# A four-layer graph kernel: two fp32 products become three rounded passes each, two tiles share a buffer, and the written-out order is redrawn

## The reference, cut to what matters

```
w  = adj * exp((x Wq0 + bq)(x Wk0 + bk)^T);  x = LN(x + (w / rowsum(w)) (x Wv0 + bv))        # attention
s  = x; s = relu(adj (s W1) + b1); s = relu(adj (s W2) + b2); s = adj (s W3) + b3            # three graph products
x  = LN(x + s)
h  = LN(relu(G x Wup + bup)); x = LN(2x + G h Wdown + b)      # G = D^-1 H B^-1 H^T, H = (adj != 0), a hypergraph layer, hidden 512
x  = LN(x + 8-head attention(x), scores times 2 adj, + bo)
```

## Time and profile before

| | |
|---|---|
| three runs | 1094.12, 1098.75 (median), 1099.09 us |
| the profiled execution | 1099.65 us, its span 1097.6 us |
| PE (TensorE) busy | 1034.2 us, 94% of the span |
| PEld (weight loads, beside PE) | 917.7 us, 84% |
| DVE (VectorE) | 796.9 us, 73% |
| ACT (ScalarE) | 683.3 us, 62% |
| POOL (GpSimd) | 481.6 us, 44% |
| DMA | 42.41 MB, 39 GB/s |

### The profile page before, as it was taken

One profiled execution on the slowest core, in us unless ns is written; L12 is line 12 of the kernel. 1 busy time (PEld: TensorE's weight loads), 2 busy tenths in 40 slices (PEclk: granted clock), 3 DMA queues, 4 the chain that ended last, 5 costly groups with the idle time before them and its releaser, 6 DMA issues.

```text
span 1097.6 us, 23273 instructions
## 1 busy us (share of the span) xinstructions
PE 1034.2 (94%) x8368; PEld 917.7 (84%) x8368; DVE 796.9 (73%) x2175; ACT 683.3 (62%) x1995; POOL 481.6 (44%) x295
## 2 busy tenths in 40 slices
PE   6789999999999999999999999999999999998755
PEld 5588888888989888898988888898988888886644
DVE  4646868778686868778686877868686877867464
ACT  3245683948577593948668494857659394855524
POOL 1225254644444364634535464434436462441504
PEclk9699999999999999999999999999999999999876
DMA  5101100101011010101001010101001010000000
GB/s 220 49 10 49 39 30 30 59 29 57 0 46 40 29 57 29 57 26 60 0 29 57 29 57 29 57 0 61 25 29 57 29 57 29 11 1 10 21 20 20
DMA packets 15009, 42.41 MB, mean 39 GB/s; under 512 B 1792, under 2 KB 1792, under 8 KB 14848
## 3 DMA queue, kind: packets, MB, share of 16 engines
q1 hardware_dynamic: 14976, 41.97, 11.4%
HBM read 33.57 MB, written 8.39 MB: 38 GB/s over the span
## 4 chain that ended last, share of the span: by engine, by line
PE 86%; ACT 6%; DVE 4%; issue 1%; POOL 1%; DMA 0%; POOLq 0%; SPq 0%; DVEq 0%
PE ps L454 79%; PE ps L763 4%; ACT pr L919 2%; PE ps L704 1%; ACT fT_high L856 1%; ACT ctxT L928 1%; DVE pr L1209 1%; PE ps L634 1%; PE ps L551 1%; DVE st L1032 0%; DVE fT_rest L1112 0%; POOL rstd L1278 0%; DMA pr<-in_weights 0%; POOL pr L1324 0%; DVE x L1048 0%
## 5 line engine op out<-in xcount | busy, mean ns | idle before, releaser
L919 ACT ACTIVATE pr<-pr,mx 128x128 f32<-128x128 f32 x512 | 201.8, 419 | 6.2 <-DVE mx L1214 6.2
L1324 POOL TENSOR_TENSOR pr<-pr,den 128x1024 f32<-128x1024 f32 x64 | 121.7, 1902 | 66.5 <-DVE den L1218 64.9
L1278 POOL TENSOR_TENSOR rstd<-var,neg_half 128x4 f32<-128x4 f32 (+1 forms) x80 | 72.9, 912 | 125.9 <-DVE var L1043 124.2
L1048 DVE TENSOR_SCALAR x<-x,mv,rstd 128x256 f32<-128x256 f32 x256 | 90.2, 418 | 39.3 <-POOL rstd L1278 39.0
L1303 POOL TENSOR_TENSOR x<-x,rows 128x1024 f32<-128x1024 f32 x16 | 38.0, 2374 | 178.1 <-PE ps L454 178.1
L919 ACT ACTIVATION_READ_ACCUMULATOR pr<-pr,mx 128x1 f32 x512 | 111.0, 217 | 0.0
L1313 POOL TENSOR_TENSOR hv<-hv,neg_half 128x2 f32<-128x2 f32 x32 | 22.5, 702 | 178.3 <-DVE hv L1175 178.2
L1032 DVE BATCH_NORM_STATS2 st<-x 128x6 f32<-128x256 f32 x256 | 93.2, 414 | 1.7
L1209 DVE TENSOR_TENSOR pr<-ps,adjB 128x1024 f32<-128x1024 f32 x64 | 75.3, 1219 | 15.7 <-PE ps L454 15.6
L873 ACT COPY s_s<-ps 128x512 f32<-128x512 f32 x32 | 18.8, 588 | 102.5 <-PE ps L454 102.5
L1122 DVE TENSOR_TENSOR ctx_rest<-ps,ctxT 128x512 fp32r<-128x512 f32 x32 | 22.2, 692 | 82.9 <-ACT ctxT L928 82.9
(11 more groups left out here) (190 smaller groups left out, 3231.1 us busy)
## 6 DMA issues: line engine op xcount, KB each, us to landing
...
```

What stands on the lines that cost most here:

```text
L919: act.activation(pr[:, b, k, :], pr[:, b, k, :], ACT.Exp, bias=mx[:, b, k:k + 1], accum_out=den[:, b, 0, k:k + 1]).then_inc(exp_ready, 1)
L1048: dve.tensor_scalar(t[:, b, :], t[:, b, :], mv[i][:, b, 0:1], rstd[i][:, b:b + 1], ALU.subtract, ALU.mult).then_inc(ready, 1)
L1278: pool.tensor_tensor(rstd[i][:, bs], var[i][:, bs], neg_half[:, bs], ALU.pow).then_inc(rstd_ready[i], len(pairs))
L1324: pool.tensor_tensor(pr[:, b], pr[:, b], den[:, b, 1, :].unsqueeze(2).broadcast_to([P, HEADS, P]), ALU.mult).then_inc(pr_ready, 1)
```

## The change

The first attention's output (`att_out`) and the third graph product (`gcn_3a`) are made from rounded parts in three passes. For that ACT's copies of `v0`, `p0T` and `s3` now write rounded tiles, DVE takes three kinds of remainders (steps `v0_rest`, `p0T_rest`, `s3_rest`), and the adjacency is split too (step `adj_split`: ACT rounds, POOL subtracts). `qkT` and `upT` become one tile, the sums of squares are formed in place, and other tiles are shared or cut. The load of the next `adjTA` moves from `gcn_3a1` to `gcn_2a`. The lists of all engines are redrawn, also where the arithmetic is unchanged. All of it in the loop's lists, and the code:

```
-IN_UPT = [("W3", C, D), ("Wv3T", C, D), ("WoT", C, D)]
+IN_V3 = [("W3", C, D), ("Wv3T", C, D)]
+IN_Y2 = [("WoT", C, D)]
...
 SCHEDULE = {
-    "PE": [("B", "gcn_3a0"), ("A", "att_t"), ("A", "att_t_rest"), ("C", "mha_xt"), ("B", "gcn_3a1"),
-        ("C", "mha_qk01"), ("C", "mha_qk01_rest"), ("C", "mha_qk2"), ("C", "mha_qk3"), ("A", "att_v0"),
+    "PE": [("B", "gcn_3a0"), ("A", "att_t"), ("B", "gcn_3a1"), ("C", "mha_xt"), ("C", "mha_qk01"),
+        ("A", "att_t_rest"), ("C", "mha_qk01_rest"), ("C", "mha_qk2"), ("C", "mha_qk3"), ("A", "att_v0"),
         ("C", "mha_scores0"), ("A", "att_v1"), ("A", "att_scores"), ("C", "mha_scores1"), ("C", "mha_v0"),
-        ("C", "mha_v1"), ("A", "att_turn"), ("B", "hyper_x"), ("A", "att_out"), ("B", "hyper_up01"),
+        ("A", "att_turn"), ("C", "mha_v1"), ("B", "hyper_x"), ("A", "att_out"), ("B", "hyper_up01"),
         ("B", "hyper_up01_rest"), ("B", "hyper_up2"), ("A", "gram"), ("B", "hyper_up3"), ("A", "gcn_ax"),
-        ("C", "mha_turn0"), ("C", "mha_turn1"), ("A", "gcn_1"), ("A", "gcn_1_rest"), ("C", "mha_ctx0"),
-        ("C", "mha_turn2"), ("C", "mha_wo0_high"), ("A", "gcn_2s1_high"), ("A", "gcn_2s0_high"), ("C", "mha_wo0"),
+        ("C", "mha_turn0"), ("C", "mha_turn1"), ("A", "gcn_1"), ("C", "mha_ctx0"), ("A", "gcn_1_rest"),
+        ("C", "mha_wo0_high"), ("C", "mha_turn2"), ("C", "mha_wo0"), ("A", "gcn_2s0_high"), ("A", "gcn_2s1_high"),
         ("A", "gcn_2s0"), ("A", "gcn_2s1"), ("C", "mha_turn3"), ("A", "gcn_2a"), ("C", "mha_ctx1"),
-        ("B", "hyper_down0_high"), ("C", "mha_wo1_high"), ("C", "mha_wo1"), ("B", "hyper_down0"),
-        ("B", "hyper_down1_high"), ("B", "hyper_down1"), ("A", "gcn_3s1_high"), ("A", "gcn_3s0_high"),
-        ("A", "gcn_3s0"), ("B", "hyper_out"), ("A", "gram_turn"), ("A", "gcn_3s1")],
+        ("B", "hyper_down0_high"), ("C", "mha_wo1_high"), ("B", "hyper_down0"), ("A", "gcn_3s1_high"),
+        ("C", "mha_wo1"), ("B", "hyper_down1_high"), ("B", "hyper_down1"), ("A", "gcn_3s0_high"), ("A", "gcn_3s0"),
+        ("B", "hyper_out"), ("A", "gram_turn"), ("A", "gcn_3s1")],
...
-        ("C", "mha_max0"), ("C", "mha_max1"), ("A", "att_exp"), ("C", "mha_scores1"), ("C", "mha_max2"),
-        ("C", "mha_max3"), ("C", "mha_div0"), ("A", "att_out"), ("B", "hyper_rest0"), ("B", "hyper_rest1"),
...
+        ("B", "x1_means1"), ("B", "x1_stats"), ("A", "incidence"), ("B", "x1_norm"), ("A", "v0_rest0"),
+        ("C", "mha_scores0"), ("C", "mha_max0"), ("A", "v0_rest1"), ("A", "att_exp"), ("C", "mha_scores1"),
+        ("C", "mha_max1"), ("C", "mha_max2"), ("A", "p0T_rest"), ("C", "mha_max3"), ("C", "mha_div0"),
+        ("A", "att_out"), ("B", "hyper_rest1"), ("B", "hyper_rest0"), ("C", "mha_div1"), ("A", "att_res1"),
...
+        ("A", "z2_rest1"), ("C", "mha_wo1"), ("B", "hyper_y0"), ("C", "x3_stats1"), ("B", "hyper_down1"),
+        ("B", "hyper_y1"), ("A", "s3_rest0"), ("B", "hyper_out"), ("B", "hyper_out1"), ("B", "x2_means0"),
+        ("B", "x2_means1"), ("B", "x2_stats"), ("A", "s3_rest1"), ("B", "x2_norm"), ("C", "x3_norm1")],
...
+        ("C", "mha_turn1"), ("C", "mha_exp3a"), ("C", "mha_ctx0"), ("A", "adj_split"), ("A", "gcn_1"),
+        ("B", "squares0"), ("B", "squares1"), ("A", "x_split"), ("A", "gcn_2s0"), ("A", "gcn_2s1"),
...
-        qkT = sb("qkT", [P, 2 * C, N4]); upT = sb("upT", [P, HC, N4])
+        qkT = upT = sb("qkT_upT", [P, HC, N4])
...
             def att_out(g):
+                pe.wait_ge(p0T_rest_ready, g + 1)
+                pe.wait_ge(v0_rest_ready, GB * g + GB)
...
-                    mm(ps[:, att_bank(b), 0:D + 1], p0T[:, b * P:(b + 1) * P], v0[:, b, 0:D + 1]).then_inc(att_done, 1)
+                    mm(ps[:, att_bank(b), 0:D + 2], p0T[:, graph(b)], v0[:, b, :], 0, 3)
+                    mm(ps[:, att_bank(b), 0:D + 2], p0T[:, graph(b)], v0_rest[:, b, :], 1, 3)
+                    mm(ps[:, att_bank(b), 0:D + 2], p0T_rest[:, graph(b)], v0[:, b, :], 2, 3).then_inc(att_done, 1)
...
             def gcn_3a(g, pair):
-                pe.wait_ge(s3_ready, 2 * g + 1 + pair)
+                pe.wait_ge(s3_rest_ready, 2 * g + 1 + pair)
+                pe.wait_ge(adj_rest_ready, g + 1)
                 for b in (2 * pair, 2 * pair + 1):
-                    last = mm(ps2[:, 2 + pair, b % 2], adjTA[:, b, :], s3[:, b, :])
+                    mm(ps2[:, 2 + pair, b % 2], adj_high[:, b, :], s_high[:, b, :], 0, 3)
+                    mm(ps2[:, 2 + pair, b % 2], adj_high[:, b, :], s_rest[:, b, :], 1, 3)
+                    last = mm(ps2[:, 2 + pair, b % 2], adj_rest[:, b, :], s_high[:, b, :], 2, 3)
...
                 if not first(g):
-                    act.wait_ge(sqs_ready, g)
+                    act.wait_ge(down_done, GB * g)
+                    act.wait_ge(s3h_done, 2 * g)
...
+            def v0_part(g, pair):
+                for b in (2 * pair, 2 * pair + 1):
+                    dve.wait_ge(v0_ready, GB * g + b + 1)
+                    dve.tensor_tensor(v0_rest[:, b, 0:D], ps[:, 2 + b % 2, 0:D], v0[:, b, 0:D], ALU.subtract).then_inc(v0_rest_ready, 1)
+
+            def p0T_part(g):
+                dve.wait_ge(p0T_ready, g + 1)
+                dve.tensor_tensor(p0T_rest[:], ps[:, 1, :], p0T[:], ALU.subtract).then_inc(p0T_rest_ready, 1)
...
+            def s3_part(g, k):
+                dve.wait_ge(s3_ready, 2 * g + k + 1)
...
+            def adj_split(g):
+                pool.wait_ge(adj_high_ready, g + 1)
+                pool.tensor_tensor(adj_rest[:], adjTA[:], adj_high[:], ALU.subtract).then_inc(adj_rest_ready, 1)
```

More of the change, by code:

```diff
@@ L62 @@
 PROLOGUE = {
-    "PE": [("set_att", 0), ("set_down", 0), ("att_t", 0), ("set_wo", 0), ("att_t_rest", 0), ("att_v0", 0),
+    "PE": [("set_att", 0), ("set_wo", 0), ("set_down", 0), ("att_t", 0), ("att_t_rest", 0), ("att_v0", 0),
         ("att_v1", 0), ("att_scores", 0), ("att_turn", 0), ("att_out", 0), ("gram", 0), ("gcn_ax", 0), ("gcn_1", 0),
         ("gcn_1_rest", 0), ("gcn_2s1_high", 0), ("gcn_2s0_high", 0), ("gcn_2s0", 0), ("gcn_2s1", 0), ("gcn_2a", 0),
-        ("gcn_3s1_high", 0), ("gcn_3s0_high", 0), ("gcn_3s0", 0), ("gcn_3s1", 0), ("gcn_3a0", 0), ("gcn_3a1", 0),
-        ("gram_turn", 0), ("att_t", 1), ("att_t_rest", 1), ("att_v0", 1), ("att_v1", 1), ("att_scores", 1),
-        ("hyper_x", 0), ("att_turn", 1), ("att_out", 1), ("hyper_up01", 0), ("gram", 1), ("hyper_up01_rest", 0),
[1 row of a table removed]
+        ("gcn_3s0_high", 0), ("gcn_3s1_high", 0), ("gcn_3s0", 0), ("gcn_3s1", 0), ("gcn_3a0", 0), ("gcn_3a1", 0),
+        ("gram_turn", 0), ("att_t", 1), ("att_v0", 1), ("att_t_rest", 1), ("att_v1", 1), ("att_scores", 1),
+        ("hyper_x", 0), ("att_turn", 1), ("att_out", 1), ("hyper_up01", 0), ("hyper_up01_rest", 0), ("gram", 1),
[1 row of a table added]
@@ L104 @@
-    "ACT": [("high_WoT", 0), ("high_W1", 0), ("x_high", 0), ("high_Wv0T", 0), ("high_att", 0), ("high_W3", 0),
-        ("high_Wv3T", 0), ("high_W2", 0), ("high_WupT", 0), ("high_WdownT", 0), ("att_t", 0), ("att_v0", 0),
-        ("high_Wqk3T", 0), ("att_v1", 0), ("att_off", 0), ("att_exp", 0), ("att_turn", 0), ("gcn_ax", 0),
-        ("gcn_1", 0), ("gcn_2s0", 0), ("gcn_2s1", 0), ("x_split", 0), ("gcn_2a", 0), ("gcn_3s0", 0), ("gcn_3s1", 0),
-        ("gram_turn", 0), ("att_t", 1), ("att_v0", 1), ("att_v1", 1), ("att_off", 1), ("att_exp", 1), ("att_turn", 1),
[10 rows of a table removed]
@@ L119 @@
-    "POOL": [("att_t", 0), ("x_rest0", 0), ("x0_stats", 0), ("x0_bias", 0), ("att_t", 1), ("x_rest", 0),
[5 rows of a table removed]
-    "SP": [("att_scores", 0), ("att_turn", 0), ("att_out", 0), ("gcn_3a1", 0), ("att_out", 1), ("att_scores", 1),
-        ("att_turn", 1), ("gcn_3a1", 1), ("att_scores", 2), ("mha_scores1", 0), ("att_out", 2), ("att_turn", 2),
-        ("x3_norm1", 0)],
[4 rows of a table added]
+        ("hyper_out", 1), ("gram_turn", 2), ("gcn_3s1", 2)],
+    "DVE": [("set_rep", 0), ("set_att", 0), ("set_reps", 0), ("rest_att", 0), ("rest_WoT", 0), ("rest_Wv0T", 0),
[24 rows of a table added]
+        ("high_WupT", 0), ("x_high", 0), ("high_Wv3T", 0), ("att_t", 0), ("high_WdownT", 0), ("att_v0", 0),
+        ("att_v1", 0), ("att_off", 0), ("att_exp", 0), ("high_Wqk3T", 0), ("att_turn", 0), ("gcn_ax", 0),
+        ("adj_split", 0), ("gcn_1", 0), ("x_split", 0), ("gcn_2s0", 0), ("gcn_2s1", 0), ("gcn_2a", 0), ("gcn_3s0", 0),
+        ("gcn_3s1", 0), ("gram_turn", 0), ("att_v0", 1), ("att_t", 1), ("att_v1", 1), ("adj_split", 1),
+        ("att_off", 1), ("att_exp", 1), ("att_turn", 1), ("hyper_x", 0), ("up_out0", 0), ("up_out1", 0),
[10 rows of a table added]
@@ L128 @@
+    "POOL": [("att_t", 0), ("x_rest0", 0), ("x0_stats", 0), ("x0_bias", 0), ("att_t", 1), ("x_rest", 0),
[6 rows of a table added]
+    "SP": [("att_turn", 0), ("att_scores", 0), ("att_out", 0), ("gcn_2a", 0), ("att_out", 1), ("att_turn", 1),
+        ("att_scores", 1), ("gcn_2a", 1), ("att_scores", 2), ("att_out", 2), ("att_turn", 2), ("mha_scores1", 0),
+        ("gcn_2a", 2), ("x3_norm1", 0)],
 }
 SCHEDULE = {
```

(24 more changed lines are left out.)

67 lines of the change are left out of this document (38 added, 29 removed), and 255 rows, old and new, of tables (EPILOGUE, PROLOGUE, SCHEDULE).

## The result

The changed kernel takes 1125.85 us (median of four, 1125.02 to 1126.99) against 1097.4 for the kernel before in the same comparison: 1.0264 times as long, 95% interval 1.0235 to 1.0292. Slower, as forecast (1120, range 1094 to 1131). The profiled execution's span is 1122.9 us against 1097.6.

What follows compares the result with a forecast made beforehand. PE's list was taken as the time, 62.12 of 62.5 us busy. Terms 1.13 + 0.9 - 0.27 gave +1.76 a period, +21 over 12 periods, 0 outside: 1120.7 from 1099.65, likeliest 1120 us, range 1094 to 1131.

Steps and rivals of the forecast that it cites:

- The products: att_out and gcn_3a in three rounded passes instead of plain fp32: together 0.52 us a period saved on PE.
- only PE's work counts: Rival: the redrawn lists keep PE fed, the period loses 1.16 us, 1085 us in all; chance 0.15.
- (a): Head of the period to mha_scores1: no filler before mha_qk01 and a later x2_norm, +1.13 us a period, lower end +0.56.
- Filler: Between mha_xt and mha_qk01 no step stands in the new list, so PE idles 0.6 to 0.7 us every period.
- The 2.55 from x2_norm: Head of the period: mha_qk01 starts 2.55 us after x2_norm starts, with nothing else in the way.
- (b): mha_scores1 to gcn_ax: remainders in DVE's stream delay att_out and x0_norm, +0.9 us a period, lower end -0.2.
- (c): gcn_ax to gcn_2s0: old wait gone, but late gcn_ax and adj_split delay ACT; -0.27 us a period, ends -0.64 and 0.
- (d): Rest of the period, after gcn_2s0: the same work in another order, 0 us.
- The loop's sum: The stretches of the loop added up: +1.76 us a period, +21 us over 12 periods.
- prologue and epilogue: 0: Outside the loop: four groups' products saved (-2 us) against remainders added in front of tighter chains (+2 us), 0 in all.
- A queue falls behind: Rival: POOL's adj_split delays squares, hyper_y and x2_norm; period +2.9 us, 1133 us; sign hyper_y1 over 1.7 after hyper_down1; chance 0.16.

Runs made afterwards that it cites:

- one_swap: The changed kernel with att_t_rest moved between mha_xt and mha_qk01 in PE's loop list: 1115.9 us, period 63.30.
- fill_oldends: The changed kernel with both products in plain fp32, att_t_rest between mha_xt and mha_qk01, and the old prologue and epilogue lists: 1094.16 us, period 62.41.
- head_old: The changed kernel with the head of PE's loop list in the order of the kernel before: 1116.84 us, period 63.30.
- gcn_fp32: The changed kernel with gcn_3a alone back in plain fp32, without s3_rest and adj_split, adjTA's load at its old place: 1121.7 us, period 63.43.
- p0T_early: The changed kernel with p0T_rest moved ahead of mha_max2 in DVE's loop list: 1127.64 us, period 64.26.
- v1_early: The changed kernel with mha_v1's copy moved ahead of mha_exp1b in ACT's loop list: 1126.03 us, period 64.02.
- max3_late: The changed kernel with p0T_rest ahead of mha_max2 and mha_max3 behind gram_scale in DVE's loop list: 1123.37 us, period 63.77.
- three_moves: The changed kernel with att_t_rest before mha_qk01, p0T_rest before mha_max2, mha_max3 behind gram_scale, mha_v1's copy before mha_exp1b: 1113.86 us, period 63.10.
- both_fp32: The changed kernel's new lists and shared tile with both products back in plain fp32, none of the new steps: 1112.56 us, period 63.16.

## Why the prediction was right, and where it was not

**The products.** Saved about as forecast: gcn_3a0 starts 0.71 before att_t, and from att_out's first pass to hyper_up01's second it is 1.80 (587.74 to 589.54) against 1.97 before; I had 1.77, with 0.1 for a longer first pass in it. With gcn_3a that is about the 0.52 a period that I took. It did not show in the time: in both rows of the table with new lists the new arithmetic costs 0.85 and 0.89 a period net of all that it saves. The rival "only PE's work counts" fell with that.

**(a)** right in size and mechanism. Filler: one_swap gives back 0.71 (0.56 to 0.7 thought), fill_oldends 0.75. The 2.55 from x2_norm: head_old. s3_rest0 in front of x2_norm is the smaller part: gcn_fp32 gives back 0.20 there.

**(b)** right in size (+0.83 for +0.9), incomplete in mechanism. I made the whole of it from DVE's stream and the remainders in it. p0T_early, v1_early and max3_late show two holds at att_out, DVE's p0T_rest and ACT's copy of mha_v1, either enough to keep 0.5. The copy's late place is in the redrawn list of ACT, mha_v1 behind att_turn and mha_exp1b where it stood ahead of both; I had priced what was added to DVE and not what moved on ACT. With both gone, x0_norm is the third (three_moves). In time, though, only DVE's stream has been shown to count with the new arithmetic: shortening it gave 0.51 of the 0.83 back (max3_late), and taking ACT's copy away besides gave nothing more at gcn_ax (15.06 against 15.04).

**(c), (d)** right to 0.1: at gcn_2s the wait at the high passes is gone, and a short one for the remainders has come, as forecast (607.25 to 607.59 in the kernel after, where passes are 0.12 apart; no view lists it), adj_split on ACT costs about a third of a microsecond there (gcn_fp32; I had 0.5 hidden in part), and the same work in another order costs nothing. The loop's sum was 0.31 a period too high, the terms' small errors all on one side.

**The step that failed is the last term, "prologue and epilogue: 0".** I set four groups' savings (-2) against their remainders (+2) and did not lay the redrawn lists of the two ends over the clock as I did in the loop. They took +7.8 between the profiled spans, and 11 by the medians (28.45 less 17.5; 8 to 15 by the interval). Of it 4.8, or 10 by the medians, are there with the old arithmetic (both_fp32), and fill_oldends gives them back (8.8 against both_fp32, between two profiles again). So most of this term is the redrawn order of the two ends. The 3.0 between the outsides of both_fp32 and after came with the remainders, which PE meets in the prologue uncovered. Waits of PE from 0 to 173 us, after:

```profile
PE ps L466 <- DVE p0T_rest L1136: 3.5, 2, 2.1
...
PE ps L466 <- DVE v_rest L1132: 1.7, 2, 1.3
```

That 3.0 is the difference of two single profiles, and is less certain than the sum. Which list entries make the rest was not tried one by one.

The clock is not the cause. Windows of the kernel before (first two lines) and after (last two), ahead of the loop and behind it, with the granted clock as the third number from the end:

```profile
0.00:178.00 178.00, 156.89 (x1041) 137.79 (x1042) 108.73 (x321) 89.13 (x216) 60.54 (x41) 0.94 0.18 61
928.00:1097.60 169.60, 131.90 (x1094) 112.96 (x1092) 107.83 (x261) 90.20 (x293) 61.10 (x38) 0.89 0.05 18
```

```profile
0.00:178.00 178.00, 149.62 (x1029) 132.07 (x1029) 113.12 (x332) 88.51 (x215) 60.00 (x43) 0.95 0.19 66
946.00:1122.90 176.90, 136.71 (x1131) 116.13 (x1129) 115.28 (x283) 91.30 (x296) 64.27 (x41) 0.91 0.04 16
```

The kernel after was granted more of the clock, and still took longer; of the first 178 us PE stood still for 7.3 more.

So 1120 against 1125.85 is the sum of two errors, -3.7 in the loop and +7.8 outside, and what is left is the difference between profile and median. That the two are of opposite sign is luck: with the loop's sum right the forecast would have been 1116, 9.5 too low, and not 5.9. The stated range, 1094 to 1131, is wide enough for both.

**"A queue falls behind"** did not happen: POOL's work grew to 31.3 of 64 us and no wait in PE's loop names it. hyper_y1 starts 1.73 after hyper_down1 (621.93 to 623.66) where I had assumed 1.7, and that was the sign to go by.

The Trainium skill ("Perfetto Trace Analysis", Identifying the Most-Contended Engine) says to optimize the engine of the highest occupancy first, and adds that for TensorE busy time is no good measure of what is left. The second half agrees with this trace: PE's busy time rose by 0.3 a period while its products got 0.5 cheaper. The first half, taken alone, is the rival that fell (the rule stands in this section, not in Optimization Strategy, under which the prediction has it).

Left open: whether some placement of the new steps lets the loop fall below 62.55. The best found with the new arithmetic is 63.10, with DVE's x0_norm holding gcn_ax and ACT's stream holding mha_ctx0; that no order does better was not shown. With the old arithmetic, fill_oldends with mha_v1's copy at its old place on ACT is the obvious next trial (up to 0.47 a period, an estimate from 15.20 against 14.73); it was not run.
